# A new instruction order in the layer loop, and a token shift by three transfers in SBUF

## The reference

```python
x = x + xattn(layernorm(x), ctx)            # 8 heads of 64, 77 context rows
y = layernorm(x)
for l in range(2):                          # the layers
    h = shift_token(y)                      # channels 128..255 come from the token before
    q, k, v = split(h @ wqkv[l])            # 3 x 512
    q, k = rotary(l2norm(q) * qs), rotary(l2norm(k) * ks)
    o = local_attention(q, k, v)            # windows of 128, each sees itself and the one before
    y = y + o @ wo[l]
    h = layernorm(shift_token(y)) * g + b
    a, gate = split(h @ w1[l] + b1)         # 682 hidden
    y = y + (a * gelu(gate)) @ w2[l] + b2
x = x + y
```

## Time and profile before

| | |
|---|---|
| median of 3 runs | 1534.05 us (1534.04 to 1535.44) |
| profiled execution, its own time | 1534.95 us |
| span of the profiled execution | 1533.1 us |
| busy PE / PEld / DVE / ACT / POOL | 94% / 83% / 74% / 61% / 49% |
| mean granted TensorE clock | 0.98 |
| DMA | 58.88 MB, mean 38 GB/s |

### The profile page before, as it was taken

The page is one execution under the profiler, slowest core; times in us unless marked ns, Lnnn a source line. Parts: engine busy times, 40 slices in busy tenths (PEclk is TensorE's granted clock), DMA queues, the critical chain, the costliest instruction groups (busy, mean ns, idle before and its releaser), DMA issues.

```text
span 1533.1 us, 33616 instructions
## 1 busy us (share of the span) xinstructions
PE 1447.2 (94%) x11808; PEld 1278.1 (83%) x11808; DVE 1129.9 (74%) x3102; ACT 937.8 (61%) x2670; POOL 746.9 (49%) x570
## 2 busy tenths in 40 slices
PE   4999999868999999999999899999999999999987
PEld 4888888746888888888888788888888888888886
DVE  3766666446788877877777778888788888888874
ACT  2766666435666666666666666666666666666661
POOL 1121121044666666665655555555555655555642
PEclk8999999889999999999999999999999999999999
DMA  6311111200000000000001010011110100001100
GB/s 195 102 55 49 51 54 41 84 29 15 24 24 24 24 24 23 23 23 23 24 26 35 16 56 24 30 39 40 31 31 31 30 30 30 30 30 33 34 24 26
DMA packets 40843, 58.88 MB, mean 38 GB/s; under 512 B 6540, under 2 KB 22448, under 8 KB 40752
## 3 DMA queue, kind: packets, MB, share of 16 engines
q1 hardware_dynamic: 40752, 57.69, 11.7%
HBM read 38.06 MB, written 16.78 MB: 36 GB/s over the span
## 4 chain that ended last, share of the span: by engine, by line
PE 66%; DVE 18%; issue 7%; ACT 4%; POOL 2%; SPq 1%; DMA 1%; DVEq 0%; POOLq 0%; ACTq 0%
PE pb L511 26%; PE pb L788 7%; PE pb L733 6%; PE pb L802 6%; PE pb L764 4%; PE pb L826 4%; DVE p_t L1371 3%; DVE p_t L1385 3%; PE pb L748 3%; DVE r_cos L1350 2%; DVE n_sq L1336 2%; PE pb L572 2%; DVE r_sin L1356 2%; PE pb L560 2%; PE pb L610 2%
## 5 line engine op out<-in xcount | busy, mean ns | idle before, releaser
L1561 POOL TENSOR_TENSOR n_inv<-n_cl,half_neg 128x16 f32<-128x16 f32 x64 | 211.2, 3300 | 199.3 <-DVE n_cl L1341 195.9
L1058 ACT ACTIVATE p_t<-p_t,s_nm 128x128 f32<-128x128 f32 (+1 forms) x512 | 226.6, 444 | 34.5 <-DVE s_nm L1371 31.8
L511 PE MATMUL pb<-h_hi,w_hi 128*128 128x256 f32 x704 | 208.7, 296 | 5.7 <-DVE h_lo L1332 3.3
L511 PE MATMUL pb<-h_hi,w_lo 128*128 128x256 f32 x704 | 199.6, 284 | 0.0
L511 PE MATMUL pb<-h_lo,w_hi 128*128 128x256 f32 x704 | 199.4, 283 | 0.0
L1566 POOL TENSOR_TENSOR r_cos<-r_cos,r_sin 128x1024 f32<-128x1024 f32 x64 | 154.7, 2418 | 89.6 <-DVE r_sin L1356 89.6
L1371 DVE CUSTOM_DVE_ANT_0 p_t<-pb,mask_t 128x128 f32<-128x128 f32 (+1 forms) x512 | 152.0, 353 | 46.3 <-PE pb L733 30.4
L1016 ACT ACTIVATE qk_sq<-pb 128x512 f32<-128x512 f32 x128 | 72.3, 591 | 184.5 <-PE pb L511 184.5
L1049 ACT ACTIVATE pt_t<-pb 128x512 f32<-128x512 f32 x192 | 113.7, 593 | 100.5 <-PE pb L748 100.4
L511 PE MATMUL pb<-wqkv_hi,xt_hi 128*128 128x512 f32 x384 | 166.5, 434 | 5.8 <-DVE r_sin L1356 4.9
L1588 POOL TENSOR_TENSOR hg_lo<-hg,hg_hi 128x256 fp32r<-128x256 f32 x192 | 139.6, 748 | 53.9 <-DVE hg_hi L1402 53.9
(11 more groups left out here) (137 smaller groups left out, 4083.9 us busy)
## 6 DMA issues: line engine op xcount, KB each, us to landing
x_cur<-y_state SPq DMA_DIRECT2D x32, 256.0 KB, 2.7
x_res<-y_state SPq DMA_DIRECT2D x32, 256.0 KB, 2.9
x_in<-x SPq DMA_DIRECT2D x16, 256.0 KB, 2.8
x_state<-x_x SPq DMA_DIRECT2D x16, 256.0 KB, 2.0
y_state<-y_x SPq DMA_DIRECT2D x16, 256.0 KB, 2.1
y_state<-x SPq DMA_DIRECT2D x16, 256.0 KB, 2.0
x_orig<-x_state SPq DMA_DIRECT2D x16, 256.0 KB, 2.8
out<-x SPq DMA_DIRECT2D x16, 256.0 KB, 2.2
```

The source lines that it names most:

```text
L511: mm = pe.matmul(dst, s, m, start=(n == 0 and k == 0), stop=(n == len(pairs) - 1 and k == 2))
L1058: e = nc.scalar.activation(pu, pu, ACT.Exp, bias=s_nm[:, j, k:k + 1], scale=-1.0, accum_out=s_sum[:, j, k:k + 1])
L1561: nc.gpsimd.tensor_tensor(n_inv[:, t], n_cl[:, t], half_neg[:], ALU.pow).then_inc(pool_inv, 1)
```

## The change

It touches the layer loop only.

- The order of all five engines within a pass is new. On TensorE the first and second pair of score groups stand together at the head of the pass, the third follows projection (0,0); `turn_h` stands behind all six feeds; the three projections of tile 1 come in the reverse order, each between two `turn_p`; `hidden` 1 to 5 stand together.
- Scores: groups 0 to 3 have banks 3, 4, 5, 6 and groups 4 and 5 have 3 and 4. `scores(1)` waits for the residual of `c` (bank 6), and no longer for the maxima of groups 0 and 1; `turn_p(0)` waits for the maxima of group 2, `weigh(0)` for those of group 3.
- The shift: `shift_down` on TensorE and `copy_shifted` on VectorE are gone. SP issues three SBUF to SBUF transfers from block 2 to block 1 of `x1` once the residual is there, and `stats_h` waits for them. A memset clears row 0 once.
- SP issues the three transfers and the load of `x_res` first, then the tail copies, the store, and last the load of `x_cur`.
- VectorE: the casts `gate_hi` 3 to 5 stand in the next pass, between the maxima; the last gate follows the residual; `norm_probs` 5 stands ahead of `squares` 1 and `rotate` 1. GpSimd: `deviation` first; `inverse_norms` ahead of `add_parts` in tile 0; `gate_lo` 2 to 4 in the pass in which the gates are made. ScalarE: `exps` at the head of the pass, the last gelu behind `copy_qk`, `out_hi` in two parts.

```diff
+SHIFT_PIECES = [(0, 112), (112, 15)]
-        QKV_PLACE = {(0, 1): 1, (0, 0): 2, (0, 2): 3, (1, 0): 4, (1, 1): 5, (1, 2): 6}
+        QKV_PLACE = {(0, 0): 1, (0, 1): 2, (0, 2): 3, (1, 2): 4, (1, 1): 5, (1, 0): 6}
-        S_BANK = [3, 4, 3, 4, 3, 4]
+        S_BANK = [3, 4, 5, 6, 3, 4]
...
+            def shift_down(c):
+
+                for first, rows in SHIFT_PIECES:
+                    sp.dma_start(x1[first + 1:first + 1 + rows, :, 1], x1[first:first + rows, :, 2]).then_inc(shift_load, 16)
+                sp.dma_start(x1[0:1, 1, 1], x1[P - 1:P, 0, 2]).then_inc(shift_load, 16)
...
+                if c is not None:
+                    sp.wait_ge(dve_x1, at(c, 1, 1))
+                    shift_down(c)
+                    if b is not None:
+                        sp.dma_start(x_res[:], one(y_dram, seq_of(b, layer))).then_inc(res_load, 16)
                 if d is not None:
                     tail_hi(d)
                     tail_lo(d)
-                if has_next(a):
-                    sp.wait_ge(pe_xt, at(a, 1, 1))
-                    sp.dma_start(x_cur[:], one(y_dram, seq_of(plus(a, 1), layer))).then_inc(cur_load, 16)
...
+                if has_next(a):
+                    sp.wait_ge(pe_xt, at(a, 1, 1))
+                    sp.dma_start(x_cur[:], one(y_dram, seq_of(plus(a, 1), layer))).then_inc(cur_load, 16)
...
-            def shift_down(c):
-
-                pe.wait_ge(dve_x1, at(c, 1, 1))
-                pe.matmul(pb[:, 6, 0:P], down_f, x1[:, 0, 2], start=True, stop=True)
-                pe.matmul(pb[:, 6, P:2 * P], down_f, x1[:, 1, 2], start=True, stop=False)
-                pe.matmul(pb[:, 6, P:2 * P], carry_f, x1[:, 0, 2], start=False, stop=True).then_inc(pe_down, 1)
...
+                elif j == 1:
+                    if c is not None:
+                        pe.wait_ge(dve_x1, at(c, 1, 1))
                 else:
-                    pe.wait_ge(dve_max, at(b, UNITS, 2 * j))
+                    pe.wait_ge(dve_max, at(b, UNITS, 2))
...
+                if u == 0:
+                    pe.wait_ge(dve_max, at(b, UNITS, 3))
...
-                    if c is not None:
-                        pe.wait_ge(dve_down, at(c, 1, 1))
+                    pe.wait_ge(dve_max, at(b, UNITS, 4))
...
-            def copy_shifted(c):
-                dve.wait_ge(pe_down, at(c, 1, 1))
-                nc.vector.tensor_copy(x1[:, :, 1], pb[:, 6, 0:2 * P].rearrange("p (t n) -> p t n", t=NT)).then_inc(dve_down, 1)
-
             def stats_h(c):
-                dve.wait_ge(dve_down, at(c, 1, 1))
+                dve.wait_ge(shift_load, at(c, 48, 48))
```

More of the change, by code:

```diff
@@ L832, in run_l @@
                 if b is not None:
[L833 to L837, removed]
+                    scores(a, b, c, 0)
+                    scores(a, b, c, 1)
                 if a is not None:
                     project(a, d, 0, 0)
+                if b is not None:
+                    scores(a, b, c, 2)
                 if d is not None:
@@ L842, in run_l @@
                     feed(c, d, 1)
+                if a is not None:
+                    project(a, d, 0, 1)
                 if b is not None:
-                    scores(a, b, 1)
+                    turn_p(a, b, d, 0)
+                if d is not None:
+                    feed(c, d, 2)
                 if a is not None:
@@ L847, in run_l @@
                 if d is not None:
[L848 to L851, removed]
                     feed(c, d, 3)
                     feed(c, d, 4)
-                if b is not None:
-                    scores(a, b, 2)
-                    turn_p(a, b, d, 0)
-                if a is not None:
-                    project(a, d, 1, 1)
-                if d is not None:
                     feed(c, d, 5)
@@ L866, in run_l @@
                     turn_p(a, b, d, 1)
+                if a is not None:
+                    project(a, d, 1, 1)
+                if b is not None:
                     turn_p(a, b, d, 2)
+                if a is not None:
+                    project(a, d, 1, 0)
+                if b is not None:
+                    turn_p(a, b, d, 3)
+                    weigh(b, c, 1 - par, 0)
                 if has_next(a):
@@ L870, in run_l @@
                 if b is not None:
[L871 to L872 removed]
+                    turn_p(a, b, d, 4)
                 if c is not None:
                     hidden(a, b, c, 0)
[L875 to L879 removed]
                 if b is not None:
@@ L1145, in run_l @@
                     copy_qk(a, 3)
+                if c is not None:
+                    gelu(c, 5, layer)
             def between(g):
@@ L1459, in run_l @@
                 if b is not None:
-                    norm_probs(b, 4)
+                    maxes(b, 5)
+                    norm_probs(b, 3)
                 if c is not None:
                     split_h_hi(c)
+                if b is not None:
+                    norm_probs(b, 4)
+                    inverse_sums(b, 5)
+                if c is not None:
                     split_h_lo(c)
                 if b is not None:
-                    maxes(b, 5)
+                    norm_probs(b, 5)
                 if a is not None:
+                    squares(a, 1)
                     rotate(a, 1, layer)
-                    squares(a, 1)
-                if b is not None:
-                    inverse_sums(b, 5)
-                if a is not None:
                     clamp(a, 1)
-                if b is not None:
-                    norm_probs(b, 5)
+                if c is not None:
+                    gate(c, 0, layer)
+                    gate_hi(c, 0)
+                if isinstance(g, int) and g == SEQS + 1:
+                    split_lo("wo1", raw_b[:, 0:IC * D].rearrange("p (c n) -> p c n", c=IC), wo_hi[:], wo_lo[:])
                 if has_next(a):
@@ L1477, in run_l @@
                 if c is not None:
-                    gate(c, 0, layer)
+                    gate(c, 1, layer)
+                    gate_hi(c, 1)
+                    gate(c, 2, layer)
+                    gate_hi(c, 2)
                 if b is not None:
@@ L1481, in run_l @@
                 if c is not None:
-                    gate_hi(c, 0)
-                if isinstance(g, int) and g == SEQS + 1:
-                    split_lo("wo1", raw_b[:, 0:IC * D].rearrange("p (c n) -> p c n", c=IC), wo_hi[:], wo_lo[:])
-                if c is not None:
-                    gate(c, 1, layer)
-                    gate(c, 2, layer)
                     gate(c, 3, layer)
-                    gate(c, 4, layer)
-                    gate_hi(c, 1)
-                    gate_hi(c, 2)
                 if b is not None:
@@ L1494, in run_l @@
                 if c is not None:
-                    gate(c, 5, layer)
-                    gate_hi(c, 3)
-                    gate_hi(c, 4)
-                    gate_hi(c, 5)
+                    gate(c, 4, layer)
                 if b is not None:
                     residual(b)
+                if c is not None:
+                    gate(c, 5, layer)
                 if isinstance(g, int) and g == SEQS - 1:
```

137 lines of the change are left out of this document (67 added, 70 removed).

## The result

The changed kernel takes 1542.68 us (1538.67 to 1545.34, four runs) beside 1534.05 us (1533.41 to 1535.44, four runs) of the kernel before on the same chip: ratio 1.0053, 95% interval 1.0033 to 1.0072. It is slower by half a per cent. 1505 was forecast, with 1497 to 1512 as the forecast's own range.

The account below looks back on a forecast made before the run. TensorE's own instruction stream was taken to set the pace inside the layers. Per item -0.77 - 0.38 + 0.10 = -1.05 us; in total -29.4 from 1534.95 gave 1505.5, forecast 1505, own range 1497 to 1512.

Parts of the forecast that it names:

- rival 1: GpSimd's add_parts 0 takes the shared port before VectorE's norm_probs 5, so hidden 1 waits; 1544 us, chance 0.15.
- the sum: Whole-kernel total of -29.4 us: -13.7 layer 0, -3 change of layer, -16.2 layer 1, +3.5 at the ends.
- Part 1: TensorE's own work per item: shift matmuls gone, 0.59 us, and two changes of kind gone, 0.18; 0.77 us less.
- my walk: One item followed from its first score matmul with TensorE at full pace; it ends at 35.3 us.
- Part 2: TensorE's wait at turn_p 5 for norm_probs 5 goes: the step of 0.50 falls to 0.12, 0.38 us less per item.
- Part 3: New waits within an item: 0.1 us at scores 1; transfers and other chains hidden with margins of 0.2 to 0.7.
- scores 1: Second score group on TensorE, now waiting for the residual: 0.1 us of waiting per item, bounds 0 and 0.3.
- the bounds of 3.3 and 4.9: Time into the item, in us, when all three shift transfers land and the statistics can start; 4.9 was taken.
- feed 5: TensorE step needing the second tail copy, landing at 11.5 against arrival at 11.7: thinnest place, 0.2 us, no wait forecast.
- The ends: Losses outside regular items: first item +1, last items +1, layer 1's weight splits +1.5 us; change of layer -3.
- What would show it: Profile signs: tail copies 35.4 us apart, norm_probs 5 at 0.7 us; prediction wrong if norm_probs 5 shows 2 or more.

Follow-up runs that it names:

- Experiment 1: Changed kernel with one wait more: GpSimd's add_parts 0 waits for VectorE's norm_probs 5; 1507.3 us, ratio 0.9819 to the kernel before.
- Experiment 5: Changed kernel with VectorE's norm_probs 5 moved one place forward, ahead of split_h_lo, no wait added; 1622.3 us, a single run.
- experiment 4: Kernel before with one wait more: GpSimd's power of tile 0 waits for VectorE's norm_probs 4; 1544.9 us, a single run.
- experiment 6: Experiment 1's kernel with the shift back on TensorE (three matmuls, VectorE's copy) in place of the three transfers; 1518.35 us, ratio 0.9895.
- Experiment 2: Changed kernel without its three shift transfers, the shift left out and the statistics waiting for the residual alone; 1536.85 us, ratio 1.0019.
- experiments 7 and 8: Experiment 1's kernel with layer 1's weight splits moved: 7 also reorders tail copies and gates in the last passes, 1501.22 us; 8 splits alone, 1498.17 us.

## Why the prediction was wrong

**The step that failed** is the race in rival 1, "GpSimd has 0.23 and the power, 3.44 to the next start (819.33 to 822.77): 3.67. VectorE wins by 0.2". VectorE's half was right: 3.5 forecast, 3.53 measured. GpSimd's was 3.11: 0.25 to the power's start, and 2.86 in place of 3.44 from there to the next start. Those 3.44 were read as work, but in the earlier trace rows they held two waits. `norm_probs` 4, with two SBUF inputs, ran on VectorE from 819.22 to 819.91, and the power, started at 819.33, took 3.36. In the new order nothing of that kind is under way when the power of tile 0 starts, and it takes 2.90 or 2.91 in every item. The other 0.13 is that the next instruction of the earlier trace rows is the product, which needs the power's result and starts 0.08 after its end, where the addition of the new order starts 0.05 before it. The 0.45 alone are twice the margin of 0.2 that the forecast stood on. Experiment 1 shows that this race made the kernel slower: without it the kernel is 1.8% faster than the kernel before. Experiment 5 shows that 0.05 us decides it, and experiment 4 that the 0.45 were a wait for VectorE. The shorter figure could have been read beforehand, from the first items of the kernel before (2.91 at 356.77).

The second fault is one of weight. The point that decides was named, with a margin of 0.2 us, the sum of six durations of one item, and given a chance of 0.15. A margin of that size says near to even.

**Rival 1** came as priced, 1544 against 1542.7, but by sizes that balance: hidden 1 waits a mean of 0.92 in layer 0 and 0.91 in layer 1, with 0.54 more at `turn_p` 5 there (forecast 1.15 and 1.8); items of 36.1 and 36.9 (forecast 36.55 and 37.2); and the change of layer and the end lost more than stood in the sum.

**Part 1, TensorE's stream**: right in kind, too small. With the race won an item is 34.98 us or less without a gap, where my walk gave 35.3. It is 1.5 to 1.6 us shorter than before in layer 0 and 1.4 in layer 1, where the sum had 1.05 and 1.25. The shift was 0.67 (experiment 6), not 0.59. Where the rest of the difference lies was not measured step by step; changes of kind that I counted as even, such as `turn_p` behind a projection, are a guess.

**Part 2, the old wait**: gone in layer 0, back in layer 1 for 0.54, because `norm_probs` 5 was held; experiment 1 doesn't have it in either.

**Part 3**: scores 1 has no wait (0.10 forecast). The statistics start 4.4 into the item above (4.2 to 4.4 in most), between the bounds of 3.3 and 4.9 and under the 4.9 taken: the two larger transfers are issued in 1.66 together and the third in 0.61, not 0.75 each. No wait for the tail transfer at feed 5 in the regular items. Experiment 2 confirms that the transfers are hidden there. All of this chain, the one that I worked on longest, was right and decided nothing.

**The ends** were mis-sized: +3.5 in the sum and -3 for the change of layer. In experiment 1 the start gives 1.8, the five items at the change of layer cost 4.4 and the end 6.0, +8.6 together. It is that and the larger gain of the items that bring 1507.3 beside a forecast of 1505, so the total was nearer than its terms. Two causes are the transfers where no TensorE work covers them (3 to 6 us by experiment 2, 9 by experiment 6) and the weight splits (experiments 7 and 8). A third, which the sum didn't have, is the clock: in the last 60 us the mean granted clock is 0.95 before, 0.91 in the changed kernel and in experiment 6, and 0.86 in experiment 1. There TensorE stands still from 1479 to 1483, and the clock is at its lower level, 0.50, from 1482 to 1492. TensorE's busy time in those 60 us is 45.5 us for 377 matmuls before and 47.2 for 363 in experiment 1; by these numbers some 3 us of the 6 at the end are clock, which is an estimate. How to mend the last passes stays open.

**What would show it** named the fault: the text said that the prediction is wrong if `norm_probs` 5 shows 2 us or more, and it shows 2.87.

## What to carry to other kernels

A duration in a trace may hold a wait. Before a race is costed with it, look at what the other user of the port was doing at its start, and take the shortest of its kind in the whole trace, not the one in the item at hand (here 2.91 in place of 3.36). Where VectorE with two SBUF inputs and a GpSimd addition like this one (2.40 us) come within half a microsecond of each other, don't leave it to chance: one semaphore wait on the side with slack was worth 35 us here, and a mere change of order made it 80 us worse. And the transfers were cheap only with the right place in SP's queue; in the irregular items they had nothing to hide behind.

## What the runs showed of the hardware that was not expected

- GpSimd's power of 128x16 doesn't hold VectorE off as its additions do: in the changed kernel two `norm_probs` took 0.69 us each (811.36 and 812.30) while a power ran from 810.56 to 813.47. It is held itself, by 0.45 us, when such an instruction is under way at its start. The additions and the product that follow it hold such an instruction to 0.54 to 0.56 us beyond their own end.
- The other way round it holds too: the addition that started at 813.42, while `split_h_lo` (813.26 to 813.92) was running, took 2.73 us; with nothing of that kind beside it, as in experiment 1, it takes 2.40. It still came ahead of `norm_probs` 5, which had been asked for later.
- Two SBUF to SBUF transfers of 112 and 15 rows were issued in 1.66 us together, and one of a single row in 0.61.
